# A gated cross-attention and mixture-of-experts layer: the first sequence's queries copied from SBUF to SBUF on three queues, the key loads shared out, the next group's query projection moved by half a slot

## What is computed

```python
def layer(x, ctx, ...):
    q = layernorm(x) @ w_q.T                 # 16 heads of 8 values
    k, v = ctx @ w_k.T, ctx @ w_v.T
    attn = softmax(q @ k.T / sqrt(8))        # per sequence and head, 128 x 77
    x = x + tanh(g_xattn) * ((attn @ v) @ w_o.T)
    y = layernorm(x)
    shared = gelu(y @ sW1 + sb1) @ sW2 + sb2
    w = softmax(y @ gW + gb)                 # 15 experts, the best 3 of each token
    routed = sum(w[e] * (gelu(y @ rW1[e] + rb1[e]) @ rW2[e] + rb2[e]) for e in top3(w))
    return x + tanh(g_ffn) * (shared + routed + y)
```

## Time and profile before

| | |
|---|---|
| time, median of 3 runs | 418.11 us |
| time of the profiled execution | 417.4 us |
| its span, first to last instruction | 415.6 us |
| PE busy in the span | 376.5 us (91%) |
| DVE, ACT, POOL busy | 301.0 (72%), 274.0 (66%), 253.1 us (61%) |
| PE in the first six of 40 slices of the span (10.4 us each) | busy 3, 5, 8, 9, 9 and 9 tenths |
| chain that ended last | PE 58%, POOL 13%, DVE 8%, issue 7%, DMA 6%, ACT 4% |

### The profile page before, as it was taken

How to read it: one execution, slowest core, us unless ns; L and a number is a source line. 1 busy time by engine, 2 the same in 40 slices (tenths; PEclk the granted TensorE clock), 3 DMA queues, 4 the chain that set the end, 5 groups by cost and what they waited for, 6 DMA issues and landing times.

```text
span 415.6 us, 12422 instructions
## 1 busy us (share of the span) xinstructions
PE 376.5 (91%) x3840; PEld 334.3 (80%) x3840; DVE 301.0 (72%) x982; ACT 274.0 (66%) x609; POOL 253.1 (61%) x250
## 2 busy tenths in 40 slices
PE   3589999999999999999899988999999999999940
PEld 1267878787878788878899987899999997999940
DVE  6356877888888889786668976778777762687863
ACT  4338889988889897878666654566666666353500
POOL 6860120176767666675988977307777774777771
PEclk9999999999999999999999999999999999999985
DMA  4659573648363649634355447756666642233322
GB/s 146 180 148 244 175 210 111 165 136 235 118 202 122 190 131 306 225 104 153 123 179 157 155 149 232 231 179 187 193 197 203 200 142 69 77 79 102 82 76 69
DMA packets 57159, 66.30 MB, mean 160 GB/s; under 512 B 9092, under 2 KB 47748, under 8 KB 57096
## 3 DMA queue, kind: packets, MB, share of 16 engines
q1 hardware_dynamic: 49656, 51.49, 41.2%
q0 software_dynamic: 6352, 13.02, 10.8%
q10 hardware_dynamic: 1088, 1.00, 0.8%
HBM read 35.82 MB, written 29.29 MB: 157 GB/s over the span
## 4 chain that ended last, share of the span: by engine, by line
PE 58%; POOL 13%; DVE 8%; issue 7%; DMA 6%; ACT 4%; SPq 2%; POOLq 0%; ACTq 0%; DVEq 0%
PE psum L1493 13%; PE psum L1352 8%; POOL k_heads L625 8%; PE psum L1369 6%; PE psum L1473 4%; PE psum L1474 3%; PE psum L1332 3%; PE psum L1475 3%; PE psum L1463 3%; DVE max_cols L911 3%; POOL q_stack L625 2%; PE psum L1299 2%; PE psum L1342 2%; DMA w_raw<-rows_by_expert 2%; PE psum L1309 2%
## 5 line engine op out<-in xcount | busy, mean ns | idle before, releaser
L563 POOL DMA_INDIRECT rows_by_expert<-xn_all,row_of x96 | 96.1, 1001 | 44.6 <-ACT probs L711 22.5
L803 ACT ACTIVATE probs<-psum,b1c 128x256 f32<-128x256 f32 x152 | 63.8, 471 | 27.5 <-PE psum L1475 26.8
L1493 PE MATMUL psum<-w_all,probs 128*128 x608 | 80.1, 275 | 0.0
L1493 PEld LDWEIGHTS psum<-w_all,probs 128*128 128x128 f32 x608 | 74.2, 191 | 0.2
L625 POOL DMA_INDIRECT k_heads<-outs_by_block,back_row x60 | 57.9, 965 | 23.8 <-issue 16.4
L711 ACT ACTIVATE probs<-psum 77x512 f32<-77x512 f32 x128 | 68.9, 590 | 2.8 <-PE psum L1352 1.5
L911 DVE TENSOR_REDUCE max_cols<-psum 128x4 fp32r<-128x312 f32 x128 | 55.1, 472 | 7.0 <-PE psum L1332 6.5
L1352 PE MATMUL psum<-q_stack,k_heads 128*77 128x128 f32 x512 | 54.3, 243 | 0.8 <-ACT q_stack L703 0.5
L1352 PEld LDWEIGHTS psum<-q_stack,k_heads 128*77 128x77 f32 x512 | 43.8, 151 | 13.0 <-issue 5.6
L1053 DVE CAST w_ring<-w 128x512 fp32r x76 | 34.5, 454 | 22.1 <-issue 21.1
L1473 PE MATMUL psum<-q_parts,w_ring 128*128 128x256 f32 x152 | 49.1, 323 | 1.1 <-DVE q_parts L1041 1.1
(11 more groups left out here) (155 smaller groups left out, 769.5 us busy)
## 6 DMA issues: line engine op xcount, KB each, us to landing
w_raw<-rows_by_expert SPq DMA_DIRECT2D x76, 128.0 KB
outs_by_block<-probs SPq DMA_DIRECT2D x76, 128.0 KB
q_stack<-q_split SPq DMA_DIRECT2D x21, 256.0 KB
q_split<-q_parts SPq DMA_DIRECT2D x7, 512.0 KB, 3.1
k_heads<-k_split SPq DMA_DIRECT2D x90, 39.0 KB
rows_by_expert<-zeros SPq DMA_DIRECT2D x27, 128.0 KB, 3.8
k_split<-w_all SPq DMA_DIRECT2D x8, 312.0 KB, 2.2
x_all<-in_x SPq DMA_DIRECT2D x8, 256.0 KB, 4.9
```

The source lines that it names most:

```text
L563: nc.gpsimd.indirect_dma_start(xd[:, :], bass.IndirectOffsetOnAxis(ap=row_of[:, r, m:m + 1], axis=0), xn2_all[:, r * GB + m // K, :], None ...
L803: nc.scalar.activation(hid[u % 2][:, c, :], psum[:, 2 + c, 0:BLK], ACT.Gelu, bias=b1c[:, bass.ds(e * CR + (CS + c), 1)]).then_inc(gelu_don ...
L1493: ins = nc.tensor.matmul(psum[:, 4 + u % 2 * 2, b * P:(b + 1) * P], hid[u % 2][:, c, b * P:(b + 1) * P], w2_all[:, bass.ds(expert_of[u] * ...
```

## The change

Sequence 0's queries no longer pass through DRAM: twelve copies of 32 partitions by 128 columns (16 KB each) go from `q_parts` straight to `q_stack`, three on ACT's queue and five on SP's as soon as the high part is there, one on SP's and three on POOL's after the low part. `scores(0, hg)` waits for its own head group's three copies. Sequences 1 to 3 still pass through DRAM, in two parts that POOL now sends (sequence 1, then 2 and 3) after its three copies, and that SP reads back as three DMAs each. Of the twelve key loads of group 0, POOL keeps four; SP has four instead of six, ACT four instead of two. `lead_k(1)` and `trail_k(1)` stand earlier, so that `send_k(1)` can go sooner. PE does `front_x(1)` after `scores(0, 1)` instead of before `scores(0, 0)`, and `front_q(1)`, with ACT's `lead_q(1)` and DVE's `trail_q(1)`, moves into slot 0.

```diff
+            def direct_q(hg, r):
+                m = r % 2
+                sp.dma_start(q_stack[r * GR:(r + 1) * GR, 0, hg, 0:S].bitcast(F32), q_parts[hg * GR:(hg + 1) * GR, m, 0:S].bitcast(F32)).then_inc(q00_in[hg], 16)
+
+            def first_q(part, cols):
+                sp.wait_ge(q0_sent[part], 16)
+                for r, m in enumerate((0, 1, 0)):
+                    sp.dma_start(q_stack[r * GR:(r + 1) * GR, 0, :, cols].bitcast(F32), qd[0].rearrange("(g p) m t -> m p g t", g=HG)[m, :, :, cols]
+                                 ).then_inc(q0_in[part], 16)
...
-            load_k(0, 0, 6)
+            load_k(0, 0, 4)
             load_x(2)
+            sp.wait_ge(q_hi_ready, 1)
+            direct_q(1, 2)
+            direct_q(2, 0)
+            direct_q(2, 2)
+            direct_q(3, 0)
+            direct_q(3, 2)
             sp.wait_ge(q_lo_ready, 1)
-            sp.dma_start(qd[0][:, 1, 0:2 * S], q_parts[:, 1, 0:2 * S].bitcast(F32)).then_inc(q0_lo_sent, 16)
-            sp.wait_ge(q0_hi_sent, 16)
-            first_q(0, 0)
-            sp.wait_ge(q0_lo_sent, 16)
-            first_q(0, 1)
+            direct_q(3, 1)
             send_k(1)
-            sp.wait_ge(q0_rest_sent, 16)
-            for r in range(3):
-                first_q(1, r)
+            first_q(0, slice(S, 2 * S))
+            first_q(1, slice(2 * S, 4 * S))
             sp.wait_ge(k_zeroed, 2)
...
             pool.wait_ge(q_lo_ready, 1)
-            pool.dma_start(qd[0][:, :, 2 * S:4 * S], q_parts[:, :, 2 * S:4 * S].bitcast(F32)).then_inc(q0_rest_sent, 16)
+            for hg in range(3):
+                pool.dma_start(q_stack[GR:2 * GR, 0, hg, 0:S].bitcast(F32), q_parts[hg * GR:(hg + 1) * GR, 1, 0:S].bitcast(F32)).then_inc(q00_lo_in[hg], 16)
+            for part, cols in enumerate((slice(S, 2 * S), slice(2 * S, 4 * S))):
+                pool.dma_start(qd[0][:, :, cols], q_parts[:, :, cols].bitcast(F32)).then_inc(q0_sent[part], 16)
             pool.wait_ge(ln1_rstd, 2)
...
-            for hh in range(2, HQ):
-                act.dma_start(k_heads[GR + hh * DK:GR + (hh + 1) * DK, 0, :, hh].bitcast(F32).rearrange("p g b k -> p g (b k)"),
-                              kd[0].rearrange("(g h p) m c -> m h p g c", g=HG, h=HQ)[0, hh]).then_inc(k_in[0], 16)
+            load_k0(0)
+            load_k0(1)
             xT_leaves(0)
+            load_k0(2)
+            load_k0(3)
             lead_q(0)
+            lead_k(1)
             act.wait_ge(q_hi_ready, 1)
-            act.dma_start(qd[0][:, 0, 0:2 * S], q_parts[:, 0, 0:2 * S].bitcast(F32)).then_inc(q0_hi_sent, 16)
+            direct_q(0, 0)
+            direct_q(0, 2)
+            direct_q(1, 0)
             apply1(1, 0, GB)
...
-            lead_q(1)
...
+                if t == 0:
+                    lead_q(1)
                 exps(t, 2)
                 exps(t, 3)
...
-                if n in (0, 2) and hg == 0:
-                    pe.wait_ge(q0_in[n // 2], 3 * 16)
+                if n == 0:
+                    pe.wait_ge(q00_in[hg], (2 if hg < 3 else 3) * 16)
+                    if hg < 3:
+                        pe.wait_ge(q00_lo_in[hg], 16)
+                elif n in (1, 2) and hg == 0:
+                    pe.wait_ge(q0_in[n - 1], 3 * 16)
...
             front_v(0)
-            front_x(1)
             scores(0, 0)
             scores(0, 1)
-            front_q(1)
+            front_x(1)
             scores(0, 2)
             scores(0, 3)
...
                 scores_t(t, 0)
                 scores_t(t, 1)
+                if t == 0:
+                    front_q(1)
```

More of the change, by code:

```diff
@@ L203, in flamingo_kernel @@
         spare_in = sem("spare_in")
-        q0_in = [sem(f"q0_{b}_in") for b in range(2)]
-        q0_hi_sent, q0_lo_sent, q0_rest_sent = (sem(f"q0_{n}_sent") for n in ("hi", "lo", "rest"))
+        q0_in = [sem(f"q0_{n}_in") for n in ("next", "rest")]
+        q0_sent = [sem(f"q0_{n}_sent") for n in ("next", "rest")]
+        q00_in = [sem(f"q00_{hg}_in") for hg in range(HG)]
+        q00_lo_in = [sem(f"q00_{hg}_lo_in") for hg in range(3)]
         q_zeroed = sem("q_zeroed")
@@ L670, in lead_q @@
                 if g == 1:
-                    act.wait_ge(q0_hi_sent, 16)
-                    act.wait_ge(q0_lo_sent, 16)
-                    act.wait_ge(q0_rest_sent, 16)
+                    for hg in range(HG):
+                        act.wait_ge(q00_in[hg], (2 if hg < 3 else 3) * 16)
+                        if hg < 3:
+                            act.wait_ge(q00_lo_in[hg], 16)
+                    for part in range(2):
+                        act.wait_ge(q0_sent[part], 16)
                 elif g >= 2:
@@ L728, in lead_w1, with load_k0, direct_q @@
                 nc.scalar.activation(w1[:, 0, chunks, :], w_raw[:, p % 2, 0:chunks.stop - p * 4, :], ACT.Copy).then_inc(w1_lead, 1)
+            def load_k0(hh):
+                act.dma_start(k_heads[GR + hh * DK:GR + (hh + 1) * DK, 0, :, hh].bitcast(F32).rearrange("p g b k -> p g (b k)"),
+                              kd[0].rearrange("(g h p) m c -> m h p g c", g=HG, h=HQ)[0, hh]).then_inc(k_in[0], 16)
+            def direct_q(hg, r):
+                act.dma_start(q_stack[r * GR:(r + 1) * GR, 0, hg, 0:S].bitcast(F32), q_parts[hg * GR:(hg + 1) * GR, 0, 0:S].bitcast(F32)).then_inc(q00_in[hg], 16)
             lead_k(0)
@@ L736, in _ @@
             act.wait_ge(k_half_zeroed, 1)
-            for hh in range(2, HQ):
-                act.dma_start(k_heads[GR + hh * DK:GR + (hh + 1) * DK, 0, :, hh].bitcast(F32).rearrange("p g b k -> p g (b k)"),
-                              kd[0].rearrange("(g h p) m c -> m h p g c", g=HG, h=HQ)[0, hh]).then_inc(k_in[0], 16)
+            load_k0(0)
+            load_k0(1)
             xT_leaves(0)
+            load_k0(2)
+            load_k0(3)
             lead_q(0)
+            lead_k(1)
             act.wait_ge(q_hi_ready, 1)
-            act.dma_start(qd[0][:, 0, 0:2 * S], q_parts[:, 0, 0:2 * S].bitcast(F32)).then_inc(q0_hi_sent, 16)
+            direct_q(0, 0)
+            direct_q(0, 2)
+            direct_q(1, 0)
             apply1(1, 0, GB)
-            act.wait_ge(q0_hi_sent, 16)
-            act.dma_start(q_stack[2 * GR:3 * GR, 0, :, 0:2 * S].bitcast(F32), qd[0].rearrange("(g p) m t -> m p g t", g=HG)[0, :, :, 0:2 * S]
-                          ).then_inc(q0_in[0], 16)
-            lead_k(1)
             nc.scalar.activation(ident_r[:], ident_sb[:], ACT.Copy).then_inc(id_ready, 1)
@@ L1081, in _ @@
             trail_q(0)
+            trail_k(1)
             shift1_of(1)
             v_leaves(0)
-            trail_k(1)
             nc.vector.memset(v_pad[:, 1], 0.0).then_inc(v_zeroed, 1)
@@ L1118, in _ @@
                 if t == 0:
+                    trail_q(1)
                     dve.wait_ge(tanh_done, 1)
```

4 lines of the change are left out of this document (removed).

## The result

The changed kernel takes 422.5 us (median of 4 runs, 420.5 to 423.7) against 418.0 us before: ratio 1.0098, 95% interval 1.0068 to 1.0127 (the quotient of the two medians is 1.0108). It is slower by about 1%. The profiled execution is the shortest of the four, 420.47 us with a span of 418.7 us, 3.1 us over the span of before, at the same mean clock (0.986 against 0.984).

A forecast was written before the change was run, and what follows sets the result against it. PE at slot 7 was taken to be tied to SP's chain, and that to POOL's memset. The profiled 417.4 us plus 2.5 at scores(8, 0) gave 419.9, or 420.6 us as a median; range 418.0 to 422.4.

The forecast's parts named there:

- Edits at nothing: Edits priced at zero, among them ACT's two further key loads, said to lie in its wait for front_q(0).
- Landing of the copies: First low direct copy into q_stack lands at 18.4 us, so scores(0, 0) starts 3.1 us earlier.
- The caveat: If the direct copies queue behind load_x(2) and land no sooner than today, nothing later in the forecast changes.
- POOL's five issues: Three copies and two sends on POOL instead of one send shift its four memsets by 2.4 us.
- SP's chain: From POOL's zeroed keys (2.4 us later) through send_q(1) (2.9 later); group 1's queries stay hidden by 0.6 us.
- ACT in slot 0: ACT waits for group 2's layernorm, starts apply1(2, 0, 2) at 29.95 and begins slot 1 about 1.35 us late.
- PE in slot 0: Slot 0 takes 4.9 us plus 1.9 for front_q(1); turn_max(1) comes at 31.8, 1.2 us later.
- Group 2's queries: A shift of 2.7 us less 0.2 of room makes scores(8, 0) start 2.5 us later than 59.42.
- the sum: Whole kernel: 417.4 us for the profiled execution plus 2.5, 419.9; on the scale of medians 420.6 us.
- POOL's free issues: Rival: POOL's added issues cost 0.2 us instead of 2.4, memsets hardly move; 418.6 us, no change; chance 0.08.
- The stream absorbs it: Rival: DMA reserve between 35 and 48 us or room at 59.42 leaves only slot 0's 1.35 us; 419.5; chance 0.27.
- The faster case: Rival: PE's head start before slot 0 survives, keeping 2.0 to 2.9 us; some 415.7 us; chance 0.07.

The follow-up runs named there:

- run 1: The changed kernel with group 0's key loads shared as before (six on SP, two on ACT): ratio 1.0003 to the kernel before.
- run 2: The kernel before with only two of group 0's key loads moved from SP to ACT, as in the change: ratio 1.0054.
- run 5: The changed kernel with ACT's key loads reordered, heads 2 and 3 ahead of heads 0 and 1: ratio 1.0050 to the kernel before.
- run 6: The changed kernel with SP's key loads reordered, heads 2 and 3 ahead of heads 0 and 1: ratio 1.0056 to the kernel before.
- run 7: The changed kernel with load_x(2) issued behind send_k(1), key loads still shared four and four: ratio 1.0038 to the kernel before.
- run 8: The changed kernel with key loads shared as before and POOL zeroing k_heads ahead of probs of slot 0: ratio 1.0024 to the kernel before.
- run 9: The kernel of run 8 with pow1(2) moved ahead of POOL's last two memsets: ratio 1.0021 to the kernel before.
- runs 8 to 12: Run 8; run 9; run 9 with send_q(1) earlier, 0.9984; the kernel before, keys zeroed first, send_q(1) earlier, 0.9989; the third with probs zeroed on DVE, 0.9990.

## Why the prediction came out as it did

The forecast was 420.6 us, slower by 0.6%, with a range up to 422.4. The median, 422.5 us, lies 0.1 above that; 1.0098 times the 418.11 us that the forecast starts from is 422.2, within it. The sign was right, and POOL's part in it. But one term was missing and one was too large, and that the two nearly made up for each other is luck.

- **Edits at nothing: the step that failed.** "ACT's two further key loads lie in its wait" is true of ACT: `lead_q(0)` starts at 13.62, no later than needed. But I counted only the issuing engine, and not what the loads do to the landing of everything else in flight. Undone, this edit gives back about 4 us of the 4.5 (run 1); done alone, beside the old trip through DRAM, it costs 2.3 (run 2). Why it costs that is open (runs 5 to 7).
- **Landing of the copies: wrong through the same edit.** I had 18.4 from the landings of POOL's key loads; it became 22.30. With the keys back five executions start at 18.48 to 20.36 (median 19.95), so the price was some 1.5 us too low by itself: POOL's copies, which I had landing after 3.1, take 3.2 to 5.0 us there (medians of the five profiles). The caveat "nothing below changes, since the start then isn't what decides" was wrong as well, since POOL's sends land late with them (6.4 us instead of the 3.5 I took from the earlier trace rows), and SP waits for these.
- **POOL's five issues: right.** Forecast +2.4, measured +2.31 (0.53 us a copy, 0.74 a send); `pow1(2)` ready at 29.72, forecast 29.7. By the rule of the Trainium skill ("DMA: Bandwidth & Descriptors", section on the anatomy of one DMA, SWDGE path) the four added issues would have been 0.2 us, an estimate; the trace disagrees, with 3.08 us for the five where the one had taken 0.74.
- **SP's chain: right in kind, bound elsewhere.** I had POOL's memset release SP at 24.6; it ended at 24.54, but SP came at 26.15. "SP has read sequences 1 to 3 back by about 24" holds only with the keys back (24.2 in run 8). `send_q(1)` went out 4.0 us late (33.34 against 29.30) and not 2.9, so group 1's queries, forecast to be there 0.6 us ahead of PE, weren't hidden: PE stood 0.45 us at `scores(4, 0)`. The profile names no releaser for that wait; `load_q(1)` was issued up to 37.96.
- **ACT in slot 0: right.** `apply1(2)` at 29.95, to the hundredth, after a wait of 1.19 us for `shift`; ACT begins slot 1 1.5 us late, forecast 1.35:

```profile
29.95 0.88 ACT L697 ACTIVATE w_all<-x_all,shift,rstd 128x128 f32<-128x128 f32 x2 [1.19 <-DVE shift L906]
...
32.66 0.58 ACT L717 ACTIVATE q_stack<-psum 4x512 fp32r<-4x512 f32 x1 [0.39 <-PE psum L1368]
```

- **PE in slot 0: too dear.** Forecast +1.9 for `front_q(1)`; from `scores(1, 0)` to `turn_max(1)` it is 32.14 - 26.23 = 5.9 us instead of 4.9. The projection's own row is as dear as I had it (2.02 us), but `front_v` in the same slot takes 1.10 us instead of 1.55. Waits don't explain the rest: the trace has PE busy for 5.91 of 5.91 us, and before for 4.87 of 4.92.
- **Group 2's queries: mis-sized.** I had `scores(8, 0)` 2.5 us later, and the time with it. It was 4.6. The change without the shared keys is run 1, and its profile, the slowest of twelve executions and with the straggling send, has 4.6 as well:

```profile
63.97 0.56 PE L1356 MATMUL psum<-k_heads,q_stack 128*128 128x312 f32 x2 [1.19 <-DMA q_stack<-q_split]
```

  Run 8, which has POOL's memsets in another order besides, shows 2.1 (61.48). So the profiles don't size this term; the ratios do. Without the shared keys the change costs 0.1 us (run 1, -0.6 to 0.9) or 1.0 us (run 8, 0.0 to 2.0), where the sum had 2.5 for just that. One reason shows in the rows: of a delay at `scores(8, 0)` 0.9 us comes back by `scores(9, 0)` (4.6 and 3.7 in the changed kernel, 2.1 and 1.2 in run 8), 0.5 of it because before PE stood 0.52 us for ACT inside slot 8, at 61.76, and after it doesn't. I looked for room only ahead of that slot. The forecast came near because the excess here stood in for part of the missing 4 us.
- **The rivals.** POOL's free issues fell. "The stream absorbs it" was nearer to the truth than the forecast for the chain it spoke of: runs 1 and 8, without the sharing, come out at 1.0003 and 1.0024, and it had 0.3%. The faster case is seen in one execution of run 9, and in no median.

## What to carry to other kernels

Moving a DMA to an idle queue is not free because the queue was idle: ask what will then be in flight at once, and which small, urgent transfers stand among it. Its price depends on these: 2.3 us here beside sends through DRAM, 4.0 beside the direct copies. A busy share says little about it (0.89 at 279 and at 112 GB/s), and a drop in GB/s doesn't say which edit made it. A head start at one engine is worth only what the next releaser (here POOL's layernorm step behind its memsets, then SP's chain) lets through; even with these shortened (runs 8 to 12) nothing was won that could be measured. And where first scores differ by 2.7 us from execution to execution, undo the edit and time it many times before believing one profile.

## What the hardware showed that was not expected

- Four and four key loads on two queues cost more than six and two: 0.54% of the kernel's time in run 2, with no byte added. Loading the same rows of DRAM on both queues at once may be part of it (runs 5 and 6: ratios of 1.0050 and 1.0056 against 1.0098, with intervals that overlap); it wasn't isolated.
- The straggling send of run 1: from 35.8 to 36.8 us only eight packets are in flight anywhere, while SP waits 4.1 us for that send. In the 1.1 us ahead of these (34.7 to 35.8) the queues show a load of instructions (packets, MB, share):

```profile
q8 instruction: 1, 0.02, 5.5%
```

  Runs 6 and 8 have one between 31.5 and 37.5 us too, but their sends had landed by about 35.0. That it holds back the send's last packets fits run 1, but it wasn't tried.
- In the first 30 us the granted clock of the windows and the durations of PE's rows don't agree. In the changed kernel the windows have 1.00 all along; in run 1 they have 0.50, the 1.2 GHz level, from 21 to 27 us. But the projection of group 1's queries takes the same time in both (first row, changed kernel; second, run 1), and about half of that in the next one (third row, changed kernel):

```profile
27.93 2.02 PE L1321 MATMUL psum<-w_all 128*128 128x512 f32 x2
```

```profile
25.68 2.02 PE L1319 MATMUL psum<-w_all 128*128 128x512 f32 x2
```

```profile
36.50 1.07 PE L1321 MATMUL psum<-w_all 128*128 128x512 f32 x2
```

  The same projection takes 1.91 us in the kernel before at 22.15, where the windows have 1.00. So what the windows say of the clock there is no reason for a difference between these kernels, and the earlier trace rows priced `front_q(1)` at the slow pace that it also had in slot 0.
- Later in the kernel a late transfer can cost PE twice. In run 5 the clock fell behind the wait of 2.27 us for group 1's queries at `scores(4, 0)`, and here the rows follow it (scores of 0.86 us instead of 0.53 in run 1; columns as above):

```profile
42.00:45.00 3.00, 1.15 (x7) 0.80 (x11) 0.72 (x4) 0.04 (x1) 0.00 (x0) 0.70 1.04 292
45.00:48.00 3.00, 3.00 (x41) 2.52 (x38) 1.67 (x8) 1.41 (x4) 1.27 (x2) 0.50 1.11 340
```

  From `scores(4, 0)` to `scores(5, 0)`, 50.42, that execution takes 6.6 us, where run 1, after a wait of 1.97 us, takes 4.2 (43.38 to 47.53) at full clock. Run 7 takes 5.6 us there after a wait of 1.99, and run 6, after 2.28 us at `scores(8, 0)`, 5.7 to `scores(9, 0)` where the changed kernel takes 4.5; the windows over these stretches have clocks of 0.82 and 0.61 (run 7, 42 to 48 us) and of 0.80 and 0.63 (run 6, 63 to 69 us). So part of what the profiles of runs 5 to 7 lose is the clock's, and run 1 shows that a wait of 2 us doesn't always bring it.
